# A language-model block on one core: VectorE's clears in small pieces, its first rotations ahead of two waits, and fewer semaphore increments

## The reference

```
params = quantum_params[token_ids.reshape(-1)]
ev = _circuit_expvals(params)                      # 3 layers of RY, RZ, CNOTs; 6 numbers per token
h = ev @ post_w.T + post_b
h = h + attention(layernorm(h))                    # 8 sequences of 512, width 192
h = h + sum over the top 2 of 8 experts: prob * (gelu(x W1 + b1) W2 + b2)
```

## Time and profile before

| | before |
|---|---|
| median of 3 runs | 381.76 us (378.64 to 385.66) |
| the profiled execution | 382.33 us, its span 380.6 us |
| PE busy | 234.4 us (62%) |
| DVE busy | 171.6 us (45%), 649 instructions |
| ACT busy | 94.3 us (25%) |
| POOL busy | 244.9 us (64%) |
| busy in the stretch 36.57 to 49.17 us | DVE 4.34 of 12.60 us |
| busy in the stretch 49.17 to 61.94 us | DVE 12.49 of 12.77 us |

### The profile page before, as it was taken

One profiled execution on the slowest core, in us unless ns is written; L12 is line 12 of the kernel. 1 busy time (PEld: TensorE's weight loads), 2 busy tenths in 40 slices (PEclk: granted clock), 3 DMA queues, 4 the chain that ended last, 5 costly groups with the idle time before them and its releaser, 6 DMA issues. The chain is left out here.

```text
span 380.6 us, 6129 instructions
## 1 busy us (share of the span) xinstructions
PE 234.4 (62%) x1590; PEld 158.5 (42%) x1590; DVE 171.6 (45%) x649; ACT 94.3 (25%) x221; POOL 244.9 (64%) x259
## 2 busy tenths in 40 slices
PE   1724930067744867673462438999999948999700
PEld 0513510023422434442231215777777726777500
DVE  5836299987466675553153274232232111322200
ACT  1002002015331344440321312342424312333100
POOL 6777700499332657777367751888888388888864
PEclk9999985555685796766555558999999996999955
DMA  7510100890000010110111111655555255555520
GB/s 217 134 16 13 14 1 0 344 373 2 0 0 2 12 52 10 55 51 13 48 48 54 59 47 20 65 65 63 63 62 58 26 58 62 63 65 58 55 27 0
DMA packets 28141, 22.61 MB, mean 59 GB/s; under 512 B 15434, under 2 KB 25546, under 8 KB 27787
## 3 DMA queue, kind: packets, MB, share of 16 engines
q0 software_dynamic: 13296, 7.95, 18.7%
q1 hardware_dynamic: 14524, 14.23, 11.7%
q10 hardware_dynamic: 288, 0.03, 0.1%
HBM read 7.25 MB, written 15.63 MB: 60 GB/s over the span
## 5 line engine op out<-in xcount | busy, mean ns | idle before, releaser
L593 POOL DMA_INDIRECT out<-up x71 | 110.3, 1554 | 40.8 <-DVE up L1249 15.7
L1640 PE MATMUL bank_b<-down,up 128*128 x426 | 87.5, 342 | 5.2 <-issue 1.5
L551 POOL DMA_INDIRECT routed<-rows,slot x64 | 62.3, 973 | 37.0 <-issue 23.1
L1640 PEld LDWEIGHTS bank_b<-down,up 128*128 128x128 f32 x426 | 69.5, 192 | 22.9 <-issue 18.9
L1249 DVE TENSOR_SCALAR up<-bank_b,up 128x192 f32<-128x192 f32 x71 | 29.7, 418 | 96.7 <-PE bank_b L1640 69.2
L421 POOL DMA_INDIRECT theta_all<-angles,ids x32 | 32.1, 1003 | 11.1 <-issue 9.4
L1381 ACT ACTIVATE up<-bank_a 128x384 f32<-128x384 f32 x71 | 31.3, 497 | 2.8 <-PE bank_a L1630 2.4
L540 POOL TENSOR_TENSOR rs<-ve,minus_half 128x16 f32<-128x16 f32 x2 | 7.4, 3711 | 36.8 <-DVE ve L1026 36.8
L1497 PE MATMUL bank_b<-queries_t,keys_t 32*128 32x512 f32 x64 | 24.3, 841 | 7.9 <-DVE nmax L1043 3.0
L1504 PE MATMUL bank_a<-keys_t,wt 32*128 32x512 f32 x64 | 26.1, 898 | 3.4 <-ACT keys_t L1276 2.0
L1570 PE MATMUL bank_a<-m,a2t 32*128 32x192 f32 x64 | 13.6, 510 | 22.7 <-ACT hres L1306 12.1
(11 more groups left out here) (396 smaller groups left out, 373.5 us busy)
## 6 DMA issues: line engine op xcount, KB each, us to landing
routed<-pad_rows SPq DMA_DIRECT2D x8, 528.0 KB, 5.0
out<-hres SPq DMA_DIRECT2D x8, 384.0 KB
down<-down_w SPq DMA_DIRECT2D x1, 2304.0 KB, 9.7
up<-up_w SPq DMA_DIRECT2D x1, 1536.0 KB
out<-up POOLq DMA_INDIRECT x71, 3.5
up<-routed SPq DMA_DIRECT2D x69, 16.0 KB
routed<-rows,slot POOLq DMA_INDIRECT x64
up<-up_w SPq DMA_DIRECT2D x1, 780.0 KB
```

The costliest lines, as they stand in the source:

```text
L551: pool.indirect_dma_start(out=routed, out_offset=bass.IndirectOffsetOnAxis(slot[:, b, k, j:j + 1], 0), in_=rows[:, b, k, j, :], in_offset= ...
L593: pool.indirect_dma_start(out=out_rows, out_offset=bass.IndirectOffsetOnAxis(xb[:, m // STEP % RING, m % STEP, DEST:DEST + 1].bitcast(I32) ...
L1640: mm = pe.matmul(bank_b[:, m % 2, 0:D], hid[:, m % STEP, c * P:(c + 1) * P], down[:, bass.ds(first + c * D, D)], start=(c == 0), stop=(c = ...
```

## The change

It has three parts.

**Small pieces.** The memsets of `ev`, `u`, `w` (8 pieces each), `spread0`, `spread1` (8 each), `pad_rows` (3), `rows` (8), `u_rep` and `w_rep` (8 each) are loops now. Each piece has its own increment, and POOL's wait for `rows_clear` counts 8.

**Order.** `reduce_angles(0)` and `rotations(0)` stand ahead of the wait for `score_done`, and so ahead of the copies that wait for `m2t_done`.

**Fewer increments.** In `set_constants`, `rotations`, `chain_products`, `matrices`, `strings`, `pairs`, `sums`, `expectations`, `chain_start`, `chain_ends`, in POOL's `pair_strings`, and in `route`, only the last instructions ahead of a join increment the semaphore. The joins stay where they were. In the circuit that leaves per piece: `rotations` 1 of 8, `matrices` 1 of 22, `strings` 3 and then 2, `pairs` 3, then 2, then 3.

```
-                cstep(dve.tensor_copy(r[:, :, 1:8:6], c0.unsqueeze(2).to_broadcast(both_rows)))
+                dve.tensor_copy(r[:, :, 1:8:6], c0.unsqueeze(2).to_broadcast(both_rows))
...
                 cstep(dve.tensor_tensor(t[:, :, 2], cos_of(c, 1, 1), sin_of(c, 1, 0), ALU.mult))
...
-            step(dve.memset(spread0[:, :, :], 0.0))
-            step(dve.memset(spread1[:, :, :], 0.0))
-            step(dve.memset(pad_rows[:, :, :], 0.0))
-            dve.memset(rows[:, :, :, :, :], 0.0).then_inc(rows_clear, 1)
+            for e in range(E):
+                step(dve.memset(spread0[:, e, :], 0.0))
+            for e in range(E):
+                step(dve.memset(spread1[:, e, :], 0.0))
+            for k in range(0, REGION // P, REGION // P // 3):
+                step(dve.memset(pad_rows[:, k:k + REGION // P // 3, :], 0.0))
+            for b in range(BATCHES):
+                dve.memset(rows[:, b, :, :, :], 0.0).then_inc(rows_clear, 1)
...
-            step(dve.memset(u_rep[:, :, :, :, :], 0.0))
-            step(dve.memset(w_rep[:, :, :, :, :], 0.0))
+            for i in range(2):
+                for j in range(TILES):
+                    step(dve.memset(u_rep[:, i, j, :, :], 0.0))
+            for i in range(2):
+                for j in range(TILES):
+                    step(dve.memset(w_rep[:, i, j, :, :], 0.0))
...
+            reduce_angles(0)
+            rotations(0)
             dve.wait_ge(score_done, 1)
             dve.tensor_tensor(form_d[0:E, 0, :, :], bank_b[0:E, 0, 0:E].unsqueeze(2).to_broadcast([E, E, E]), delta,
                               ALU.mult).then_inc(score_spread, 1)
-            reduce_angles(0)
             dve.wait_ge(m2t_done, 1)
...
-            for part in circuit_parts[0:5]:
+            for part in circuit_parts[1:5]:
                 part(0)
```

More of the change, by code:

```diff
@@ L465, in pair_strings @@
[L465 to L469, removed]
+                pool.tensor_tensor(b[:, 3, :, 0], r[:, 0, 2:4], r[:, 1, 2:4], ALU.mult)
@@ new lines, in pair_strings @@
+                pool.tensor_copy(b[:, 0:3, 0, 0], r[:, 3:6, 2])
+                pool.tensor_tensor(odd[:, 1:5:3, 1], r[:, 0:3:2, 1], r[:, 1:4:2, 1], ALU.mult)
+                pool.tensor_copy(odd[:, 0, 1], r[:, 0, 1])
+                pool.tensor_tensor(h[:, 0:2], r[:, 1, 1:2].to_broadcast(two), r[:, 0, 2:4], ALU.mult)
+                pool.tensor_tensor(h[:, 2:4], r[:, 1, 2:3].to_broadcast(two), r[:, 0, 1:4:2], ALU.mult)
+                pool.tensor_tensor(e[:, 0, 0], r[:, 0, 2], r[:, 2, 2], ALU.mult)
@@ L479, in pair_strings @@
[L479 to L489, removed]
@@ new lines, in pair_strings @@
+                pool.tensor_tensor(la[:, 0], d2[:, 0:2].unsqueeze(1).to_broadcast(four),
+                                         r[:, 1].rearrange("p (a b) t -> p a b t", a=2)[:, :, 2:4], ALU.mult)
+                pool.tensor_tensor(la[:, 1, :, 0], d2[:, 2:5:2], r[:, 1, 3:8:4], ALU.mult)
+                pool.tensor_tensor(la[:, 1, :, 1], d2[:, 3:4].to_broadcast(two), r[:, 1, 2:7:4], ALU.mult)
+                pool.tensor_tensor(la[:, 2, :, 0], t[:, 1, 2:3].to_broadcast(two), r[:, 1, 1:4:2], ALU.mult)
@@ L618, in _ @@
             step(dve.memset(form_d[:, :, :, :], 0.0))
-            step(dve.memset(ev[:, :, :], 0.0))
-            step(dve.memset(u[:, :, :], 0.0))
-            step(dve.memset(w[:, :, :], 0.0))
+            for t in range(0, T, TILES):
+                step(dve.memset(ev[:, t:t + TILES, :], 0.0))
+            for t in range(0, T, TILES):
+                step(dve.memset(u[:, t:t + TILES, :], 0.0))
+            for t in range(0, T, TILES):
+                step(dve.memset(w[:, t:t + TILES, :], 0.0))
             step(dve.memset(var2_w[:, :, :], 0.0))
@@ L667, in set_constants @@
             def set_constants(n):
[L668 to L670 removed]
+                dve.memset(of(bloch, n)[:, :, 0:7:6], 1.0)
+                dve.memset(of(parity, n)[:, :, 0], 1.0)
+                dve.memset(of(tails, n)[:, 4:6], 1.0)
                 cstep(dve.memset(of(last_t, n)[:, 4], 0.0))
@@ new lines, in matrices @@
+                dve.tensor_tensor(first[:, :, 1, :, 1], r[:, 0, 0:5:4].unsqueeze(2).to_broadcast([P, 2, 2, n]),
+                                        r1[:, :, :, 1], ALU.mult)
+                dve.tensor_tensor(b[:, 3, :, 0], r[:, 0, 2:4], r[:, 1, 2:4], ALU.mult)
+                dve.tensor_copy(b[:, 0:3, 0, 0], r[:, 3:6, 2])
+                dve.tensor_tensor(of(parity, n)[:, 1:5:3, 1], r[:, 0:3:2, 1], r[:, 1:4:2, 1], ALU.mult)
+                dve.tensor_copy(of(parity, n)[:, 0, 1], r[:, 0, 1])
@@ new lines, in strings @@
+                dve.tensor_tensor(tl[:, 1], r[:, 3, 1], tl[:, 2], ALU.mult)
+                dve.tensor_tensor(lv, r[:, 5, 1:4:2], tl[:, 0:1].to_broadcast(two), ALU.mult)
+                dve.tensor_tensor(e[:, 1:5, 7], r[:, 2:6, 3], b[:, :, 0, 0], ALU.mult)
+                dve.tensor_tensor(e[:, 0, 4], of(first_h, n)[:, 1], r[:, 2, 2], ALU.mult)
+                dve.tensor_tensor(la[:, 0], d[:, 0:2].unsqueeze(1).to_broadcast(four),
+                                        r[:, 1].rearrange("p (a b) t -> p a b t", a=2)[:, :, 2:4], ALU.mult)
```

284 lines of the change are left out of this document (137 added, 147 removed).

## The result

The changed kernel took 391.1 us (median, 389.85 to 400.86), the kernel before 382.69 (378.64 to 385.66) beside it: a ratio of 1.032, 95% interval 1.027 to 1.037. It is slower, where 375.0 had been forecast.

What follows compares the result with a forecast made beforehand. DVE's circuit 0 for the first four batches was taken to bound the head. Order -2.7, fewer increments -9.4, remaining joins +4.9 sum to -7.2 from 382.33: forecast 375.0, range 368.5 to 382.5.

Steps and rivals of the forecast that it cites:

- What bounds the kernel: Head: PE and ACT wait for DVE's circuit 0; each microsecond DVE gets through it earlier moves the rest forward equally.
- The reading of the stretched starts: DVE during the gathers: an increment is served every 0.70 or 1.40 us, about eight may be outstanding; 1.05 us each.
- -9.4 + 4.9: Fewer increments: matrices(0) takes 3.2 us instead of 12.6 (-9.4); remaining joins in matrices, strings and pairs give back 4.9.
- rival C: matrices(0): the 0.7 us steps come with place or time, not increments; 379.6, or 382 if held until 48.45; chance 0.15.
- Small pieces, "cost 0": DVE's head: 67 memsets instead of 9 cost 0, within 0.3 us either way, covered by the gather of the angles.
- E: DVE's head: the pieces' 58 further increments are served slowly, from 10.6 on; +11.8, 394; chance 0.08.
- The order, -2.7: reduce_angles(0) and rotations(0) ahead of the waits: matrices(0) starts at 33.88 instead of 36.57, -2.7 us.
- D: Copies of mt: m2t_done arrives later still because DVE is busy in front of it; 378; chance 0.10.
- The sum: Whole kernel: -2.7 - 9.4 + 4.9 = -7.2 from the profiled 382.33, giving 375.1, stated as 375.0.
- B: DVE's increments are no longer served slowly, being too few to queue up; the +4.9 falls away: 370.2; chance 0.23.
- The base of the forecast: Whole kernel: the profiled execution of 382.33 us and three runs between 378.64 and 385.66, median 381.76.

Runs made afterwards that it cites:

- q1_quiet: Changed kernel with all 67 pieces, but only the last piece of each buffer increments (9 increments instead of 67); late condition: 392.84 us beside 381.13 (1.024).
- r1_pieces: Kernel before with the small pieces only (67 increments), old order, all increments in the circuit; late condition: 389.95 us beside 381.17 (1.020).
- r2_late: Changed kernel with only u_rep and w_rep in pieces (16), the other seven buffers cleared in one instruction each; 384.13 us beside 381.17 (1.017).
- q2_large: Changed kernel with the nine large clears back, new order and fewer increments kept; late condition: 382.83 us beside 383.40 (1.004).
- q3_fewest: Kernel before with the fewer increments and 17 increments less in DVE's head, large clears, old order; late condition: 381.17 us beside 383.40 (0.990).
- s1_split: Kernel before with the fewer increments, POOL's second sixteen gathers held back until matrices(0) is done, reduce_angles(1) moved later; 370.11 us beside 381.17 (0.972).
- g2_incs: Kernel before with the fewer increments only (large clears, old order); prompt condition: 356.67 us (1.000).
- f1_after: The changed kernel as it is, measured again in the prompt condition: 358.14 us beside 356.31 (1.006).
- h4_held: Kernel before with DVE held at the end of its head by 17 further clears of w_rep, each with its join; prompt condition: 373.11 us beside 356.65 (1.044).
- e2_pieces: Kernel before with the small pieces only (67 increments), old order; prompt condition: 355.95 us beside 356.21 (0.999).
- e4_order: Kernel before with the new order only; prompt condition: 357.80 us beside 356.21 (1.004).
- h1_fewest: Kernel before with the fewer increments and 17 increments less in DVE's head, large clears, old order; prompt condition: 356.07 us beside 356.49 (0.998).

## Why the prediction was wrong, point by point

The start of the main stages on DVE, from the timelines (late condition unless marked):

```
kernel              lqk copies  matrices(0)  strings(0)  w      median
before                20.42       36.57        49.17     77.20  382.7
changed               38.96       56.14        59.14     87.18  391.1
q1_quiet              41.10       56.37        59.38     87.44  392.8
r1_pieces             37.51       54.54        57.56     85.61  390.0
r2_late               26.11       48.54        51.56     79.60  384.1
q2_large              22.35       34.39        48.54     76.58  382.8
q3_fewest             18.88       34.32        49.02     77.07  381.2
s1_split              20.56       32.65        35.67     69.58  370.1
g2_incs (prompt)      19.65       31.24        34.28     62.80  356.7
f1_after (prompt)     18.89       32.11        35.11     63.90  358.1
```

- **What bounds the kernel** was right. w follows strings(0) by 28.0 us in every late run but s1_split (which waits for its angles), and h4_held put a price of one on each us of the head.
- **The reading of the stretched starts was the step that failed.** The forecast said "an increment is served every 0.70 or 1.40 us", and costed fewer increments at -9.4 + 4.9. q1_quiet, q2_large and q3_fewest stretch instructions that increment nothing, by the same 0.7 and 1.4. The price is on the instructions, not on their increments. It is not on every one: from 27.47 to 35.30 nineteen instructions of the kernel before ran while gathers were issued, and apart from the waits for PE none was held (the earlier trace rows has some of them); in matrices(0) it begins behind the eighth. That part of the reading, some eight that may be outstanding, no run contradicts, if instructions are counted and not increments: eight at 1.05 us are 8.4, an estimate from rows 4, and the changed kernel waits 8.32 us behind its last piece, r1_pieces 9.70, q1_quiet 9.71. That "the window simply holds DVE until 48.45" stood in rival C, at 382, with a chance of 0.15 for C as a whole; q2_large (382.8) and q3_fewest (381.2) are that case. Rows 4 could not tell the two readings apart, since every instruction there had an increment.
- **Small pieces, "cost 0"**, was right for their own time (e2_pieces, 355.95 against 356.21) and wrong where completions are late: there the pieces alone cost 8.8 us (r1_pieces), 67 instructions in the place of 9. This is the term that turned the sign. The sentence that should have carried weight was E's: it was given 0.08, on the strength of clears that stand 0.16 apart in the kernel before, where they are few and long. E had the signs (gaps between the pieces, a wait ahead of the lqk copies) and nearly the size (394), for the wrong reason, the increments, and with an onset at 10.6 where the trace shows 16.6 to 17.
- **The order, -2.7**: matrices(0) starts at 34.39 in q2_large, 2.2 before the old 36.57 (the copies of mt start 0.5 later than before, at 33.59: D, in part). But the stretch ends between 48.2 and 48.7 in all seven traces in which the gathers are not held back, whatever runs in it, so the 2.2 do not pass it. Nor does its end move with the last gather, which ends between 43.6 and 45.3 in them. In the prompt condition the order costs 1.6 (e4_order), where the copies of mt lose the cosine's wait as their cover and a gather is stretched; the forecast counted the copies' 0.80 only against m2t_done, which is late in one condition alone.
- **The sum** therefore was of the wrong kind. What counts in the late condition is how much work DVE has left at 48.5. Before: from strings(0) on. Changed: from reduce_angles(0) on, which is angles to cosine 53.85 - 49.01 = 4.8, rotations and copies 2.3, matrices 3.0, together 10.1; strings(0) is 9.97 later.
- **B, D** did not arise in the changed kernel: the stretch was not shorter, and m2t_done was there when rotations(0) was over, since both came behind 48.6. q2_large and q3_fewest speak against B: with one increment in matrices(0) it took 14.1 and 14.7 us.
- **The base of the forecast**: one trace and three times, all in one condition. In the other one the same change gives 1.006 (f1_after).

**Open.** What makes a completion late. The gathers' own landings are not late (the sixteenth lands before 24.9 in both conditions: q3_fewest starts on the angles at 24.87, g2_incs at 24.89). Every execution here carries its record of instructions, so no run tells whether an instruction is held back by the work or by handing in its record. The Trainium skill, page "NOTIFIC — the notification-queue block", section "7.1 Overflow: three behaviours, one of which stalls the engine", says that inside this block a producer is held back rather than a record lost; no run here shows whether that is at work. What sets the condition was not seen either; it stayed for all the runs of a job. s1_split was not run in the prompt condition; there its later angles may cost. In the late condition each kernel has one trace, and four to ten executions.

## What to carry to other kernels

An instruction is not free because it is short and covered: while GpSimd issues gathers, and in the late condition, each one on DVE beyond the first few can cost 0.7 to 1.4 us, so large clears belong in one instruction (or ahead of the gathers, which was not tried). Before stretched starts are put down to their increments, look for one without an increment in the same stretch, or make one. And where a stretch ends with another engine's work, count what is left behind its end, and move that other work first: holding back sixteen gathers brought 11 us (with fewer increments, which by themselves brought nothing that could be measured).

## What the runs showed of the hardware that was not expected

- The same program takes 356 or 382 us on one chip, minutes apart, in a condition that stays for all runs of a job; the late one shows starts 0.7 or 1.4 us apart on DVE between about 17 and 48.7 us, and signals of PE 3.3 to 12.6 us late in the head (s1_split: PE done at 22.88, DVE goes on at 26.20; r2_late: 30.34 and 42.90).
- Late signals do not come with the gathers alone: in all eight traces of the late condition ACT waits 6.9 to 12.1 us ahead of a `context_t` in the attention, between 155 and 202 us, with the releaser "remote" (10.6 in the kernel before, at 182.79, while GpSimd issues scatters of rows). No gather is left then. In the twelve traces of the prompt condition DVE and ACT have no such wait of 3 us or more between 70 and 210 us.
- In the late condition seven to nine instructions of DVE run on behind a join before the first is stretched (`own`, `both` and 5 to 7 pieces of u_rep in the changed kernel, q1_quiet and r1_pieces), with or without increments.
- Increments of DVE are free in the prompt condition: h1_fewest 0.998 (0.996 to 1.000).
- A gather of 0.95 us takes 3.1 to 3.7 in the prompt condition where the copies of mt and matrices(0) follow rotations(0) without a gap.
